# One-core macaron block (FFN, linear attention, FFN): loosened waits, new orders on all engines, and the W_v product of four second FFNs in three fp32r passes

## The reference, cut to what matters

```
def ffn(x):                       # x_prev is x shifted by one token, zeros in front
    xr = mu_r * x + (1 - mu_r) * x_prev
    xk = mu_k * x + (1 - mu_k) * x_prev
    return sigmoid(xr @ W_r) * (square(relu(xk @ W_k)) @ W_v)

def attention(x):                 # 16 heads of 16, no softmax, not causal
    q, k = relu(proj(Wq)) / 4, relu(proj(Wk)) / 4
    v, u = proj(Wv), silu(proj(Wu))
    out = srms_norm(q @ (k.T @ v)) * u
    return out @ Wo.T

x = x + 0.5 * ffn(layernorm(x))
x = x + attention(layernorm(x))
x = x + 0.5 * ffn(layernorm(x))
```

## Time and profile before

| what | value |
|---|---|
| time before, median of 3 runs | 336.86 us (336.38 to 337.03) |
| time of the profiled execution | 336.23 us |
| its span in the trace | 334.5 us |
| PE busy | 322.1 us, 96% of the span, 1916 matmuls |
| DVE, ACT, POOL busy | 71%, 66%, 46% |
| mean granted TensorE clock | 0.999 |

### The profile page before, as it was taken

How to read it: one execution, slowest core, us unless ns; L and a number is a source line. 1 busy time by engine, 2 the same in 40 slices (tenths; PEclk the granted TensorE clock), 3 DMA queues, 4 the chain that set the end, 5 groups by cost and what they waited for, 6 DMA issues and landing times. The chain is left out here.

```text
span 334.5 us, 5418 instructions
## 1 busy us (share of the span) xinstructions
PE 322.1 (96%) x1916; PEld 285.4 (85%) x1916; DVE 236.6 (71%) x559; ACT 222.2 (66%) x436; POOL 152.6 (46%) x187
## 2 busy tenths in 40 slices
PE   6899989999999999999999998999999999999996
PEld 6787879879888888888988986889898989899885
DVE  3999993584656737767593687655978787879743
ACT  3799937829749469479056355448686869598861
POOL 5487855516428147155117014112372828284660
PEclk9999999999999999999999999999999999999999
DMA  7950000000000000000000000000010101011013
GB/s 229 352 174 0 3 0 2 1 0 2 0 1 3 0 2 0 0 2 0 2 1 1 2 0 0 2 0 2 0 66 0 64 2 63 1 65 64 31 35 125
DMA packets 11035, 10.83 MB, mean 32 GB/s; under 512 B 768, under 2 KB 11008, under 8 KB 11008
## 3 DMA queue, kind: packets, MB, share of 16 engines
q1 hardware_dynamic: 10432, 10.23, 9.4%
q10 hardware_dynamic: 576, 0.26, 0.3%
HBM read 6.29 MB, written 4.19 MB: 31 GB/s over the span
## 5 line engine op out<-in xcount | busy, mean ns | idle before, releaser
L687 DVE SCALAR_TENSOR_TENSOR mix<-psA,mu,mix 128x512 f32<-128x512 f32 x64 | 44.1, 743 | 13.0 <-ACT mix L438 13.0
L319 POOL TENSOR_TENSOR mix_k_lo<-mix,mix_k_hi 128x512 fp32r<-128x512 f32 x30 | 39.9, 1351 | 19.7 <-ACT mix_k_hi L456 19.7
L438 ACT ACTIVATE mix<-psA,one_mu 128x511 f32<-128x511 f32 x64 | 39.6, 699 | 0.7 <-PE psA L960 0.7
L941 PE MATMUL psRV<-ffn_hi,mix_r_hi 128*128 128x256 f32 x128 | 36.4, 284 | 0.0
L425 ACT ACTIVATE xn<-xs,shiftA,rstdA 128x256 f32<-128x256 f32 x60 | 31.8, 607 | 6.6 <-POOL shiftA L303 6.6
L942 PE MATMUL psRV<-ffn_lo,mix_r_hi 128*128 128x256 f32 x128 | 35.7, 279 | 0.0
L943 PE MATMUL psRV<-ffn_hi,mix_r_lo 128*128 128x256 f32 x128 | 35.7, 279 | 0.0
L707 DVE TENSOR_TENSOR mix_r_lo<-mix,mix_r_hi 128x512 fp32r<-128x512 f32 x30 | 28.6, 991 | 5.9 <-ACT mix_r_hi L456 5.6
L1052 PE MATMUL psK<-k_tok,xs 128*128 128x256 f32 x128 | 29.3, 382 | 2.5 <-DVE silu_u L731 2.5
L512 ACT ACTIVATE q_store<-psX 128x512 f32<-128x512 f32 x16 | 9.6, 599 | 33.2 <-PE psX L943 33.2
L1052 PEld LDWEIGHTS psK<-k_tok,xs 128*128 128x128 f32 x128 | 23.8, 190 | 6.3 <-issue 3.3
(11 more groups left out here) (138 smaller groups left out, 897.0 us busy)
## 6 DMA issues: line engine op xcount, KB each, us to landing
xs<-x_dram SPq DMA_DIRECT2D x7, 512.0 KB, 8.7
out_dram<-xs SPq DMA_DIRECT2D x7, 512.0 KB, 2.9
out_dram<-xs SPq DMA_DIRECT2D x4, 128.0 KB, 1.7
xs<-x_dram ACTq DMA_DIRECT2D x2, 128.0 KB, 2.8
xs<-x_dram SPq DMA_DIRECT2D x2, 128.0 KB, 2.6
silu_u<-w_ffn_k_dram SPq DMA_DIRECT2D x1, 256.0 KB, 4.4
silu_u<-w_ffn_r_dram SPq DMA_DIRECT2D x1, 256.0 KB, 5.9
ffn_v_plain<-w_ffn_v_dram SPq DMA_DIRECT2D x1, 256.0 KB, 6.1
```

The lines of the kernel that those rows point to most:

```text
L319: nc.gpsimd.tensor_tensor(mix_k_lo[:, h, :], mix[:, 0, h, :], mix_k_hi[:, h, :].bitcast(F32), ALU.subtract).then_inc(s_lo_k, 1)
L438: nc.scalar.activation(mix[:, rk, h, 1:BLOCK], psA[:, h, 0:BLOCK - 1], ACT.Copy, scale=one_mu[:, rk, h:h + 1]).then_inc(s_prev, 1)
L687: nc.vector.scalar_tensor_tensor(out=m, in0=psA[:, h, :], scalar=mu[:, rk, h:h + 1], in1=m, op0=ALU.mult, op1=ALU.add).then_inc(s_mix, 1)
L941: nc.tensor.matmul(dst, a_hi, b_hi, start=start, stop=False)
```

## The change

It has these parts.

1. For n = 8 to 11 (`SPLIT2 = 12`) the W_v product is `ffn_v(n)`, three fp32r passes, instead of `ffn_v2(n)`. ScalarE squares twice (once into `act_hi`, once in place into `act_k`), and GpSimd subtracts (`act_low2`). In those steps `add_ffn2(n-1)` stands behind `k_low(n+1)`.
2. `gram` waits for `silu_u` of three tiles and for `k_tok` tile by tile; `q_of` and `transpose_b` wait by halves; `k_and_u(7)` waits for `g_acc` only ahead of its third tile.
3. `r_low(n+1)` on VectorE moves from between the tiles of `projections` to behind `stats_b(n)`, ahead of `keep_g(n-1)`. ScalarE takes the four `sigmoid_u` in a row, then `mix_high` and `normalize`. `normalize(8)` moves behind `front(7)`.
4. Steps 7 and 8 on PE: `attend(3)`, `transpose_g(2)`, `gram(7)`, `project_out(2)`. On VectorE `stats_a(9)` stands ahead of `keep_g(6)`.
5. Opening: the load of W_k of attention comes ahead of block 1 of x; 4 instead of 20 transposes after `transpose_a(0)`; the mean of each weight by itself, k before `ffn_k(0)`, v behind `ffn_r(0)`; VectorE normalizes three tiles of block 0 from mean and `rstdA` directly; the statistics of block 1 move behind the first `mix_one`; ScalarE activates the halves of step 0 around `mix_high` and `normalize(1)`; VectorE centers u, q, v behind `mix_current(1)` and makes `r_low(1)` ahead of the second half of `gate_ffn(0)`; GpSimd makes `k_low(1)` ahead of all three `att_lo`.

The core of the diff:

```
+        SPLIT2 = 12
+        xn_vector = {0: (0, 1, 2), LAST: (2, 3)}
@@ sync
+            sp.dma_start(raw_att[:, 0, :, :], weight_rows("k")).then_inc(s_w_in["k"], 16)
             load_x(1)
@@ gpsimd
+            def act_low2(n):
+                for h in range(HALVES):
+                    pool.wait_ge(s_act, 2 * (n - NB) + h + 1)
+                    nc.gpsimd.tensor_tensor(act_lo[:, h, :], act_k[:, h, :], act_hi[:, h, :].bitcast(F32),
+                                            ALU.subtract).then_inc(s_act_lo, 1)
...
-            weights_low((0,))
             k_low(1)
-            weights_low((1, 2))
+            weights_low((0, 1, 2))
...
             for n in range(8, LAST):
-                if n - 5 < NB:
+                if n < SPLIT2:
                     norm_second(n - 5)
-                if n > 8:
+                    act_low2(n)
+                    if n > 8:
+                        scales_a(n + 2)
+                    k_low(n + 1)
+                    if n > 8:
+                        add_ffn2(n - 1)
@@ scalar
+                    if n < SPLIT2:
+                        nc.scalar.activation(act_hi[:, h, :], act_k[:, h, :], ACT.Square).then_inc(s_act_hi, 1)
+                        act.wait_ge(s_act_hi, 2 * n + h + 1)
                     nc.scalar.activation(act_k[:, h, :], act_k[:, h, :], ACT.Square).then_inc(s_act, 1)
...
+            ffn_weight_high(1)
+            ffn_weight_high(2)
+            activate_k(0, (0,))
             mix_high(0, 1)
-            activate_k(0)
             normalize(1)
-            ffn_weight_high(2)
-            att_weight_high(0)
+            activate_k(0, (1,))
             previous(1)
...
-                sigmoid_u(i - 1, 1)
+                for t in range(1, TILES):
+                    sigmoid_u(i - 1, t)
                 mix_high(i + 1, 1)
-                sigmoid_u(i - 1, 2)
-                if 1 < i <= 5:
-                    normalize(i + 2, tiles=(0, 1))
-                sigmoid_u(i - 1, 3)
-                if 1 < i <= 5:
-                    normalize(i + 2, tiles=(2, 3))
+                if i <= 5:
+                    normalize(i + 2)
@@ vector
             mix_current(1)
+            center_weight("u", 3)
+            center_weight("q", 3)
+            center_weight("v", 4)
             gate_ffn(0, 0)
             add_ffn1(0, 0)
+            r_low(1)
             gate_ffn(0, 1)
             add_ffn1(0, 1)
-            r_low(1)
             stats_b(0)
...
                 stats_b(i)
+                r_low(i + 1)
                 keep_g(i - 1)
@@ tensor
             def gram(a):
-                pe.wait_ge(s_kt, 4 * a + 4)
-                pe.wait_ge(s_silu, 4 * a + 4)
+                pe.wait_ge(s_silu, 4 * a + 3)
                 for f in range(HALVES):
                     for t in range(TILES):
+                        if f == 0:
+                            pe.wait_ge(s_kt, 4 * a + t + 1)
...
-            keep_clock_up(20)
+            keep_clock_up(4)
+            weight_mean("k")
             pe.wait_ge(s_ffn_lo[0], 1)
             ffn_k(0)
-            weight_means(0)
-            weight_means(1)
+            weight_mean("u")
+            weight_mean("q")
             transpose_a(1)
             pe.wait_ge(s_ffn_lo[1], 1)
             ffn_r(0)
+            weight_mean("v")
...
             gram(6)
-            pe.wait_ge(s_gacc, 7)
             k_and_u(7)
+            attend(3, [(s_halo, 10)])
             transpose_g(2, [(s_silu, 30)])
-            attend(3, [(s_halo, 10)])
+            gram(7)
             project_out(2)
-            gram(7)
...
                     project_out(j)
-                    ffn_v2(n)
+                    ffn_v(n)
```

More of the change, by code:

```diff
@@ L207, in mix_part, with normalized @@
             return 4 * n + (2 * rk + h if n == 0 else 2 * h + rk) + 1
+        xn_vector = {0: (0, 1, 2), LAST: (2, 3)}
+        def normalized(n, t):
+            vector = t in xn_vector.get(n, ())
+            tiles = sorted((m, u) for m in range(n + 1) for u in range(TILES)
+                           if (u in xn_vector.get(m, ())) == vector)
+            return (s_xn0 if vector else s_xn), tiles.index((n, t)) + 1
         def prev_part(n, rk, h):
@@ L295, in scales_a @@
                 if n > 0:
-                    pool.wait_ge(s_xn, 4 * n - 2)
-                    pool.wait_ge(s_xn0, 2)
+                    for t in range(TILES):
+                        pool.wait_ge(*normalized(n - 1, t))
                 pool.wait_ge(s_mvA, n + 1)
@@ L417, in att_weight_high, with normalize @@
                                      ACT.Identity).then_inc(s_att_hi, 1)
-            def normalize(n, tiles=range(TILES)):
+            def normalize(n):
                 b = FFN[n][1]
@@ L423, in normalize @@
                     act.wait_ge(s_tA, 2 * n)
-                for t in tiles:
+                for t in range(TILES):
+                    if t in xn_vector.get(n, ()):
+                        continue
                     nc.scalar.activation(xn[:, t, :], tile_row(xs, b, t), ACT.Identity,
@@ L456, in mix_high, with activate_k @@
                     nc.scalar.activation(hi[:, h, :], mix[:, rk, h, :], ACT.Identity).then_inc(done, 1)
-            def activate_k(n):
-                for h in range(HALVES):
+            def activate_k(n, halves=range(HALVES)):
+                for h in halves:
                     act.wait_ge(s_k, 2 * n + h + 1)
@@ L532, in _ @@
             ffn_weight_high(0)
-            normalize(0, tiles=(0, 1))
-            ffn_weight_high(1)
+            normalize(0)
             first_column(0)
@@ L631, in _ @@
                 if n + 2 <= LAST:
-                    normalize(n + 2, tiles=(0, 1))
+                    normalize(n + 2)
             activate_k2(LAST)
@@ L661, in stats_a, with bn_all @@
                     dve.wait_ge(s_x_in[b], 16)
+                for t in tiles:
+                    if n == 0:
+                        dve.wait_ge(s_x0[t], 16)
+                    nc.vector.bn_stats(statsA[:, t, :], tile_row(xs, b, t)).then_inc(s_bnA, 1)
+            def bn_all(n):
                 if n > 0:
@@ L842, in _, with act_low_first @@
             ffn_weight_low(1)
+            center_weight("k", 1)
             stats_a(2)
-            center_weights(0)
-            for h in range(HALVES):
+            ffn_weight_low(2)
+            def act_low_first(h):
                 dve.wait_ge(s_sq, h + 1)
@@ L1065, in kv, with q_of @@
                 last.then_inc(s_kv, 1)
-            def q_of(a, free):
-                for s, v in free:
-                    pe.wait_ge(s, v)
+            def q_of(a, freed):
+                s, v = freed
                 for m in range(HALVES):
+                    pe.wait_ge(s, v - 1 + m)
                     for c in range(HALVES):
@@ L1109, in project_out, with weight_mean @@
                         last.then_inc(s_wo, 1)
[L1111 to L1119 removed]
+            def weight_mean(name):
+                pe.wait_ge(s_w_in[name], 16)
+                if name == "v":
+                    pe.wait_ge(s_wcen, 1)
+                w = wv[:] if name == "v" else raw_att[:, ATT_W.index(name)]
+                for c in range(HALVES):
+                    last = nc.tensor.matmul(mean_of(name), mean_w[:], w[:, c, :],
+                                            start=(c == 0), stop=(c == HALVES - 1))
                 last.then_inc(s_wmean, 1)
@@ L1149, in _ @@
             gram(0)
-            q_of(0, [(s_silu, 2)])
+            q_of(0, (s_silu, 2))
             for i in range(2, 5):
@@ L1169, in _ @@
             attend(0, [(s_halo, 8)])
[L1170 removed]
+            q_of(4, (s_silu, 18))
             ffn_k(6, [(s_gacc, 5)])
@@ L1181, in _ @@
             attend(1, [(s_halo, 9)])
-            q_of(5, [(s_x2, 2)])
+            q_of(5, (s_x2, 2))
             ffn_k(7, [(s_gacc, 6)])
@@ L1191, in _ @@
             attend(2, [(s_gu, 4)])
-            q_of(6, [(s_x2, 4)])
+            q_of(6, (s_x2, 4))
             transpose_a(8, [(s_gu, 6)])
```

104 lines of the change are left out of this document (50 added, 54 removed).

## The result

| what | value |
|---|---|
| time after, median of 4 runs | 328.17 us (328.04 to 328.43) |
| time before, beside it on the same chip (4 runs) | 336.78 us |
| ratio | 0.9746, 95% interval 0.973 to 0.9763 |
| profiled execution, its span | 328.15 us, 326.3 us |

The change makes the kernel 8.6 us faster. The prediction was 6.5 us faster, 330.4 us with a range from 328.6; the time lies 0.4 us under that range. The direction was right, and so were most of the places in which time went; several of the sizes were not.

What follows compares the result with a forecast made beforehand. The prediction took PE, busy for 96% of the span, as the bound. Its terms, -2.5 - 4.4 - 0.5 + 0.9 = -6.5 us, gave 329.7 us from the profiled 336.23, or a 330.4 us median, range 328.6 to 333.4 us.

Steps and rivals of the forecast that it cites:

- What bounds the kernel: PE, busy 96% of the span; only less PE work or less of its 12.4 us idle time helps.
- Term 1: W_v product of steps 8 to 11: three passes save 0.63 us a step, 2.5 us together, at worst 1.7.
- Term 2: PE's listed waits at gram, k_and_u, transpose_g and q_of go: 4.4 us saved, bounds 2.9 and 4.4.
- Term 3: Opening: ffn_k(0) starts earlier, transpose_b(0) waits for xs; 0.5 us saved, from 1.0 us loss to 1.5 us gain.
- Term 4: Steps 10 to 12: GpSimd's additions stretch mix_r_lo, so transpose_g waits; 0.9 us lost, bounds 0 and 3.3.
- A: Rival: the opening becomes a new bound and the first grams still wait; 332.9 us, chance 0.13.
- B: Rival: VectorE and GpSimd's shared access eats the split's saving in steps 10 to 12; 332.8 us, chance 0.09.
- C: Rival: squares or act_lo come late, or grams only change what they wait for; about 332.8 us, chance 0.08.
- D: Rival: slower, mix_r_lo and GpSimd wait for each other wherever it moved, delaying ffn_k; 344.3 us, chance 0.05.
- more than the sum: Case that waits behind the listed ones fall away too, gaining beyond the forecast; chance 0.03.

Runs made afterwards that it cites:

- e7: The changed kernel with the additions to xs at the head of GpSimd's steps 9 to 11: 326.82 us.
- e3: The kernel before with PE's loosened waits and the new orders of steps 1 to 8, opening and second FFNs as before: 329.87 us.
- e2: The kernel before with the new orders of ScalarE and VectorE in steps 1 to 8, PE's waits and order as before: 331.80 us.
- e5: The changed kernel with gram(1), gram(2) and gram(3) made to wait for both halves of gate_ffn: 330.18 us.
- e4: The changed kernel with the opening of the kernel before: 327.73 us.
- e10: The changed kernel with the opening of before and the additions to xs at the head of GpSimd's steps 9 to 11: 327.35 us.
- e12: The changed kernel with the additions to xs at the head of GpSimd's steps and 28 instead of 40 warm-up transposes: 326.07 us.
- e14: The changed kernel with the opening of before, the additions at the head of GpSimd's steps and 28 instead of 40 transposes: 327.12 us.
- e9: The kernel before with the split of steps 8 to 11 alone: 334.72 us.

## Why the prediction was right or wrong, point by point

**What bounds the kernel: right, with one slip.** The 16.06 us that I called an average of four steps are what steps 9, 10 and 11 take each; step 12 takes 15.25. Nothing in the sum rests on it.

**Term 1, the split: right.** Forecast -2.5 us. With the new wait taken away (e7), steps 8 to 12 take 76.94 instead of 79.40 us: -2.46 us. The saving is spread over three groups: in step 9 `project_out` takes 3.27 instead of 3.46 us, the W_v product 3.02 instead of 3.27, and `ffn_k(10)` behind it 2.80 instead of 2.97. So the distance from `project_out` to `ffn_k` fell by 0.44 us and not by 0.6, and the rest lies inside `ffn_k`; the sum, 0.61 us, is what I took from rows of other groups. The squares on ScalarE and the subtractions on GpSimd cost nothing, as argued.

**Term 2, the loosened waits: mis-sized, and this is the step that failed.** Forecast -4.4 us, measured -6.8. The waits went where I said, and nothing took their place: `g_acc` ends 1.15 us ahead of `ffn_k(3)` (forecast 1.1). But I summed the idle rows, 4.4 us, and called that sum the upper bound; e3 measured 6.8 us. A row counts the gap from the modelled end of the matmul ahead. Without a gap PE does not wait for that end. The kernel before:

```profile
66.60 0.28 PE L943 MATMUL psRV<-ffn_hi,act_lo 128*128 128x256 f32 x1
67.57 3.69 PE L1052 MATMUL psK<-k_tok,xs 128*128 128x256 f32 x16 [0.69 <-DVE silu_u L731]
70.91 0.59 PE L941 MATMUL psX<-x_hi,att_hi 128*128 128x512 f32 x1
```

and the changed one:

```profile
66.21 0.28 PE L989 MATMUL psRV<-ffn_hi,act_lo 128*128 128x256 f32 x1
66.32 3.61 PE L1100 MATMUL psK<-k_tok,xs 128*128 128x256 f32 x16
69.58 0.59 PE L987 MATMUL psX<-x_hi,att_hi 128*128 128x512 f32 x1
```

From the start of the last pass to that of `gram` it was 0.97 us and is 0.11: 0.86 us for a row of 0.69. In the changed kernel `gram` starts at 66.32, before the modelled end of the pass ahead (66.49). `gram` itself took 3.34 us and takes 3.26; I have no cause for these 0.08 us. Together the gap cost 0.94 us.

Over the nine gaps of the earlier trace rows rows of 4.4 us cost 6.75 us of distance, 0.26 us more each. e2 shows the same on two of them (0.25 and 0.31 us more) and e5 on the gaps that it adds (0.23). The surplus is an average, not a constant. In steps 2 to 5 the two groups around the gap show 0.25, 0.23, 0.23 and 0.14 us. The distance of step 5 shows only 0.03, since its `ffn_r` ran in 2.81 us before and in 2.91 us after. The gap of `transpose_g(2)` (0.41 us) cost most: `attend` and `project_out` behind it took 2.02 and 3.56 us before, and 1.78 and 3.46 in e2, which has the same order on PE and no such gap.

PE's busy time tells the same story. It fell by 5.0 us: by 2.2 us between `ffn_k(2)` and `ffn_k(8)`, where the change took no work away, by 2.0 us in steps 8 to 12 and by 0.8 us in the opening. The 2.2 us are the surplus of the gaps there, which the profile books as busy time. I had the cause at hand ("the distance between two starts is what a group of them occupies on PE") and still priced the gaps by rows.

**Term 3, the opening: wrong in its cause.** Forecast -0.5 us. With 40 transposes the runs don't settle its size: +0.4 us by e4 against the changed kernel, but -0.5 us by e10 against e7, the same pair with the additions moved. The steps up to `ffn_k(2)` are 0.2 us longer with it, and the start varies by more. I had the wait of `transpose_b(0)` right in its cause, and too long: 1.16 us for 1.8. I had `ffn_k(0)` hang on `mix_one`'s place behind the statistics. It hangs on `transpose_a(0)`, and that on the last of 40 warm-up transposes. Counted from the start of `transpose_a(0)`, `ffn_k(0)` came 3.71 instead of 4.10 us later; but that start lay at 9.46 in this profile and at 8.74 before. A part of this 4.10 is a wait for tiles that were not ready: in e4, with the same opening and the start at 9.03, it is 3.85 us. What the edit gave is rather that the tiles are ready at 8.1 instead of 9.05 us, and the warm-up hid it. e12 to e14 show the mechanism. No rival of mine named this case: work that is ready before PE comes to it.

**Term 4, the new wait: right in its mechanism, half the size.** Forecast +0.9 us, measured +0.5 (e7). `norm_second` starts 5.48 us after `ffn_k(10)` instead of 4.65, 0.8 us later and not 1.1: `mix_r_lo` took the 1.1 us longer (2.54 for 1.43), but it started 0.2 us earlier in its step, 13.62 instead of 13.80 us after `ffn_k(9)`. The Trainium skill's rule from SBUF - State Buffer, "Who interferes with whom", that I weighed there, agrees with what this run shows: additions that read two tensors stretch `mix_r_lo` as the subtractions do, 2.54 us against 1.45 without them.

**The sum.** -2.46 - 6.8 + 0.4 + 0.5 = -8.4 us by the runs' terms, against 8.6 measured, with the +0.4 us of term 3 uncertain as said. Of the difference to my -6.5 us, term 2 alone makes 2.4 us, and term 4 another 0.4. The rivals: A is refuted (no gram waits), B by e7 and e9, C by PE's busy time, which fell by 5.0 us with 3.2 us less idle time, D by e3, where `ffn_k` waits for no `g_acc`. The 0.03 for "more than the sum" was too little: no term could grow by my bounds, because I took a row's length for the most that a gap can cost.

## What to carry to other kernels

Price a gap on a busy PE by the distance between the starts around it, against the same pair of groups where no gap stands, and not by the idle row: here nine gaps cost half as much again as their rows. When work is readied earlier, look at what the waiting engine does until then; a warm-up of fixed length can be what it is late for (28 instead of 40 transposes gave 1.2 us). The fastest version measured is the changed kernel with the additions at the head of GpSimd's steps and 28 transposes: 326.07 us.
